# Linear attention's masked scores times values, and attention scores over 32 rows, in single precision without split operands

## The chip, the cores and the metric

The kernel runs on one core of one Trainium2 chip. The metric is the device time of one execution in microseconds, lower is better. All times here come from executions on the chip.

## The reference, cut to what matters

64 batches, each with 64 tokens of 256 features, pass three layers with residual connections: cross attention over a context of 256 rows (16 heads of 16), a gated linear attention (16 heads, keys of 8, values of 16), and a mixture of seven experts and a shared one. The change touches the first two.

```
q, k, v = heads((ln(x) @ Wq + bq)), heads(ctx @ Wk + bk), heads(ctx @ Wv + bv)
attn = softmax(mask(rope(q * 16 ** -0.5) @ rope(k).T))
x = x + (attn @ v) @ Wo + bo
# linear attention, per head and step
state = state * g[..., None] + k[..., :, None] * v[..., None, :]
out = q @ state
x = x + (silu(ln(x) @ Wg + bg) * norm(out)) @ Wo
```

The linear attention is computed in chunks: decayed scores q.k within the 64 steps of a batch, masked to the lower triangle, times the values.

## The kernel before, in words

Each engine has its own hand-written program, and semaphores tie them together. Two batches make a pair, and there are 32 pairs. In one step of the loop every engine does, in an order written out by hand, a part of the attention of pair p, of the linear attention of pair p - 1 and of the projections of pair p + 1. TensorE's order in a step is: scores(p, 0), the turn of the normalised rows for linear attention, the turn of the next context, g_project, project_kv 0, g_gate (the product on line 719 with 16 rows), project_kv 1 to 3, turn_probs(p, 0), g_scores (line 857), turn_xn, weigh_values(p, 0), scores(p, 1), project_q, g_values (line 869), turn_heads(p, 0), turn_k (line 757), turn_probs(p, 1), g_turn_out, weigh_values(p, 1), turn_q (line 777), g_project_out, turn_heads(p, 1), project_out, g_turn_x2, g_logits. Line 714 is every single precision transpose, line 719 every product without split operands, line 727 every split product. After the pairs come the experts, with other code.

A product with split operands has both operands as a half precision high part and a half precision rest: high times high, high times rest, rest times high. Plain operands are single precision, for which the trace shows two records a matmul (one a transpose).

The attention scores (lines 782 to 799). For half b of a pair, four bf16 matmuls put the mask into the four banks ps[:, 0..3, :] (line 788). Then, for two groups g, two parts of the query and four banks r, a matmul over 64 rows (line 796). The 64 rows are two heads, each with the key's high part and its rest side by side; the query's operand holds the high part twice (part 0) or the rest twice (part 1). The query's operand is masked by head parity, so that one matmul gives two heads' scores. What makes those operands:

- key: DVE adds the two rotary products (line 1442), ScalarE casts the high part (k_high, line 1123), GpSimd subtracts the rest (split_k, line 604), TensorE turns 16 half precision blocks (line 757), ScalarE copies two tiles of 128x1024 (k_copies, a helper line, 1104).
- query: DVE adds (line 1456), ScalarE casts twice side by side (q_high, line 1134), DVE subtracts (q_low, line 1460), TensorE turns 8 blocks (line 777), DVE masks the high part in two instructions (line 1470), ScalarE masks the rest (q_low_turned, line 1144).

Masked scores times values in linear attention. DVE masks the scores into a_t in four instructions (line 1584), ScalarE casts a_s[0] (line 1226), GpSimd subtracts a_s[1] (split_a, line 610). DVE makes the values' high part (line 1517) and their rest (line 1522), with the gate's sum between them (line 1519). TensorE does 16 heads x 3 products x 2 batches (line 869), each 64x64 weights and 16 columns. ScalarE copies the result out and undoes the scales of the halves (line 1234), which releases DVE's statistics (lines 1604 to 1621).

GpSimd's step is: residual, masks_of, rope_k (line 591), split_a, split_k, rope_q (line 619), split_v (line 599), split_x2. DVE's step after line 1584 is: line 1442, normalise(p, 0) (lines 1482 and 1490), the gate times its inverse (line 1593), max_rows(p, 1) (line 1416), q_bias (lines 1447 and 1450), the statistics (1604 to 1621), probs_low(p, 1) (line 1476), line 1460, normalise(p, 1), line 1470, and then the sum x2 (line 1635) and its statistics. ScalarE's step after line 1226 is: a copy, line 1123, the exponentials of half 1 and rank 0 (line 1163), the copy on line 1234, the other exponentials with heads_copy between them, lines 1243 and 1246, probs_high(p, 1) (helper line 1104) with line 1134 in its middle, a copy, k_copies, heads_copy, line 1144, the logarithm and exponential of x2's normalisation (lines 1109 and 1112).

Of the kernel before, what the change touches and what calls it, by code (L numbers as in the profile page):

```python
# [51 lines left out]
V_SCALE = 2.0 ** 4  # L52
A_SCALE = 2.0 ** 6
# [14 lines left out]
def constants():  # L68
# [27 lines left out]
    put("gla", (np.arange(SQ)[None, :] >= (p % SQ)[:, None]) * (A_SCALE / W_SCALE ** 2))  # L96
# [65 lines left out]
def program(nc, stack, x, ctx_in, pad, xWq, xbq, xWk, xbk, xWv, xbv, xWo, xbo, gWq, gWk, gWg1, gWg2, gWv,  # L162
# [40 lines left out]
    def halves(k, n):  # L203
# [13 lines left out]
    ident_h1 = place(P // 2).bitcast(F16)  # L217
# [11 lines left out]

    k_s = k_swap.rearrange("p t n -> p (t n)").bitcast(F16).rearrange("p (t h s c) -> p t h s c", t=4, h=8, s=2)  # L230
    k_t = place(4 * 2 * SK // 2).bitcast(F16).rearrange("p (m b j) -> p m b j", m=4, b=2)
# [5 lines left out]

    q_s = q_both.bitcast(F16).rearrange("p (s h r c) -> p s h r c", s=2, h=8, r=2)
    q_t = [place(4 * 2 * 2 * SQ // 2).bitcast(F16).rearrange("p (m b a i) -> p m b a i", m=4, b=2, a=2)
           for _ in range(2)]  # L240
# [12 lines left out]
    g_v_s = halves(1, D)  # L253
# [18 lines left out]
    a_s = [h.rearrange("p r (h c t) -> p r h c t", h=4, c=NCH) for h in halves(4, 4 * NCH * CH)]  # L272
# [82 lines left out]
    for name in """  # L355
# [5 lines left out]
        exp_done probs_turned probs_hi_ready probs_lo_ready v_split v_hi_ready a_hi_ready k_hi_ready k_split q_hi_ready q_split q_lo_t_ready g_v_hi_ready av_done inv_ready av_ready  # L361
# [8 lines left out]
        silu_ready hid_ready down_done y_ready a_split gla_hi_ready gla_lo_ready gs_step decay_step  # L370
# [160 lines left out]
    def _(pool):  # L531
# [5 lines left out]
        nc.gpsimd.tensor_copy(ident_h1, ident).then_inc(S["fill_ready"], 1)  # L537
        pool.wait_ge(S["fill_ready"], 2)
# [62 lines left out]
        def split_k(j):  # L601

            wait(pool, S["k_hi_ready"], j.n(1, 1))
            nc.gpsimd.tensor_tensor(k_s[:, :, :, 1, :], k_rot.rearrange("p t (h c) -> p t h c", h=8),
                                    k_s[:, :, :, 0, :], ALU.subtract).then_inc(S["k_split"], 1)

        def split_a(g):

            wait(pool, S["a_hi_ready"], g.n(1, 1))
            nc.gpsimd.tensor_tensor(a_s[1], a_t, a_s[0], ALU.subtract).then_inc(S["a_split"], 1)  # L610

# [17 lines left out]
        def step(p, nxt=True, gla=True):  # L629
            residual(p)  # L630
            if nxt:
                masks_of(p.next())
                rope_k(p.next())
            if gla:
                split_a(p.next(-1))
            if nxt:
                split_k(p.next())
                rope_q(p.next())
                split_v(p.next())
            if gla:  # L640
                split_x2(p.next(-1))
# [4 lines left out]
        split_k(Step(0, 0))  # L646
# [9 lines left out]
        split_a(Step(0, NPAIR - 1))  # L656
# [52 lines left out]
    def _(pe):  # L709
# [40 lines left out]
        def turn_k(j):  # L750
            wait(pe, S["k_split"], j.n(1, 1))
            for g, bank in enumerate((bank_tb, bank_mb)):
                out = bank.bitcast(F16)
                for m in range(2):
                    for t in range(4):
                        at = (4 * m + t) * P
                        ins = pe.transpose(out[:, at:at + P], k_s[:, t, 4 * g + 2 * m:4 * g + 2 * m + 2, :, :]
                                           .rearrange("p h s c -> p (h s c)"), ident_h1)
                ins.then_inc(S["k_turned"], 1)
# [11 lines left out]
        def turn_q(j):  # L771
            wait(pe, S["q_split"], j.n(1, 1))
            out = bank_ta.bitcast(F16)
            for s in range(2):
                for m in range(4):
                    at = (4 * s + m) * P
                    ins = pe.transpose(out[:, at:at + P],
# [1181 lines left out]
```

## Time and profile before

| | us |
|---|---|
| median of 3 runs | 2202.21 |
| lowest and highest run | 2198.93, 2202.3 |
| the profiled execution | 2206.32 |
| its span, first to last instruction | 2204.5 |
| TensorE busy (matmuls) | 1762.0 (80%) |
| VectorE (DVE) busy | 1489.1 (68%) |
| ScalarE (ACT) busy | 1048.1 (48%) |
| GpSimd (POOL) busy | 746.0 (34%) |
| mean granted TensorE clock, share of full | 0.887 |

PE is TensorE's matmul, PEld its weight load, DVE VectorE, ACT ScalarE, POOL GpSimd. L869 is line 869 of the kernel. In a timeline a row merges neighbouring instructions of one kind: start, length from the first start to the last end, engine, line, operation, what it writes and reads, the count, and in brackets the idle time before it with the releaser. A row of matmuls holds one record for half precision and two for a single precision product. DVE's rows of several instructions overlap a little with the next.

### The profile page before, as it was taken

Reading aid. Unit: us, or ns where it says so; the run is one execution under the profiler, and the core shown is the slowest. Engines: PE = TensorE matmul, PEld = TensorE weight load, DVE = VectorE, ACT = ScalarE, POOL = GpSimd, SP = SyncE. Lnnn points to the kernel's source line nnn. Section 1 sums busy time; section 2 is a strip of 40 time slices with the busy share of each in tenths; the row PEclk is TensorE's granted clock in tenths of the full one; section 3 lists DMA queues with packets and bytes.
Section 4 is the critical chain, followed back from the end, with each engine's and each line's share of the span. In section 5 each row is a group of like instructions: output and inputs, shape, how many; then the busy total and the mean of one; then the engine's idle time right before and its main releaser. Section 6 shows DMA issues by size and latency. Waiting matters only on the chain.

```text
span 2204.5 us, 50620 instructions
## 1 busy us (share of the span) xinstructions
PE 1762.0 (80%) x19164; PEld 1298.4 (59%) x19164; DVE 1489.1 (68%) x2913; ACT 1048.1 (48%) x2616; POOL 746.0 (34%) x850
## 2 busy tenths in 40 slices
PE   5777877787777777877787777656588999999997
PEld 3554555555555555555555555435466888888876
DVE  3777787778877787787877877746554444444446
ACT  2655555555655565555655565532243222222221
POOL 3434333333334332433243324214601333333320
PEclk8988988988889898888889888868889999999999
DMA  3100100010001000100010000003243222222352
GB/s 98 55 17 17 32 17 17 17 32 17 17 17 32 17 17 17 33 17 17 17 32 17 18 17 19 4 3 101 85 114 80 73 71 70 69 72 69 72 178 95
DMA packets 118233, 98.28 MB, mean 45 GB/s; under 512 B 67728, under 2 KB 106272, under 8 KB 118000
## 3 DMA queue, kind: packets, MB, share of 16 engines
q1 hardware_dynamic: 95376, 46.26, 8.3%
q0 software_dynamic: 10752, 33.17, 4.3%
q10 hardware_dynamic: 11872, 15.60, 2.5%
q8 instruction: 163, 2.67, 0.5%
q14 instruction: 70, 0.57, 0.1%
HBM read 62.49 MB, written 18.35 MB: 37 GB/s over the span
## 4 chain that ended last, share of the span: by engine, by line
PE 43%; DVE 16%; issue 6%; ACT 4%; POOL 3%; ACTq 1%; DMA 1%; DVEq 0%; SPq 0%; POOLq 0%
PE ps L1011 15%; PE ps L719 7%; PE ps L1038 7%; PE ps L727 5%; PE ps L714 5%; POOL experts L663 3%; DVE experts L1416 2%; DVE work L1398 2%; DVE experts L1426 1%; ACT experts L1144 1%; PE ps L857 1%; DVE experts L1442 1%; ACT work L1104 1%; PE ps L1043 1%; DVE experts L1584 1%
## 5 line engine op out<-in xcount | busy, mean ns | idle before, releaser
L1011 PE MATMUL ps<-work,experts 128*128 128x256 f16 x3564 | 417.8, 279 | 51.2 <-ACT work L1303 23.4
L1011 PEld LDWEIGHTS ps<-work,experts 128*128 (+1 forms) x3564 | 348.6, 100 | 111.8 <-issue 37.4
L714 PE MATMUL ps<-cst,experts 128*128 128x128 f32 x1376 | 238.6, 313 | 104.9 <-DVE experts L1476 56.7
L1104 ACT ACTIVATE experts<-ps 128x512 f16<-128x512 f32 (+3 forms) x416 | 253.6, 646 | 71.4 <-PE ps L714 67.8
L719 PE MATMUL ps<-experts 128*128 128x512 f32 (+1 forms) x640 | 281.9, 581 | 4.0 <-DMA experts<-in_L_xattn_bv 3.3
L714 PEld LDWEIGHTS ps<-cst,experts 128*128 128x128 f32 x1376 | 177.0, 160 | 155.7 <-issue 91.8
L1163 ACT ACTIVATE experts<-ps,experts 128x256 f32<-128x256 f32 x512 | 235.1, 474 | 64.3 <-DVE experts L1416 64.3
L1104 ACT ACTIVATE work<-work 128x768 f16<-128x768 f32 x108 | 90.9, 842 | 339.0 <-PE ps L1043 216.7
L591 POOL TENSOR_TENSOR experts<-experts,cst 128x128 f32<-128x128 f32 x256 | 135.2, 564 | 281.8 <-DVE experts L1426 281.8
L1038 PE MATMUL ps<-experts,work 128*128 (+1 forms) x1620 | 196.5, 274 | 3.7 <-DVE work L1703 3.7
L719 PEld LDWEIGHTS ps<-experts 128*128 128x128 f32 x640 | 119.8, 200 | 120.2 <-issue 103.4
L1476 DVE TENSOR_TENSOR experts<-ps,experts 128x512 f16<-128x512 f32 x256 | 165.5, 683 | 35.6 <-ACT experts L1104 33.1
L1038 PEld LDWEIGHTS ps<-experts,work 128*128 128x128 f16 x1620 | 154.5, 98 | 28.5 <-DVE work L1703 4.1
L673 POOL DMA_INDIRECT work<-token_in,work x76 | 73.9, 972 | 272.5 <-DMA work<-work 252.7
L1686 DVE SCALAR_TENSOR_TENSOR work<-ps,work 128x768 f32<-128x768 f32 x108 | 88.9, 824 | 111.7 <-ACT work L1303 55.9
L1416 DVE TENSOR_REDUCE experts<-ps 128x2 f32<-128x512 f32 x256 | 159.0, 684 | 4.6 <-PE ps L796 3.4
L1104 ACT ACTIVATE work<-ps 128x128 f32<-128x128 f32 (+2 forms) x160 | 55.5, 347 | 194.6 <-PE ps L714 194.6
L1426 DVE TENSOR_TENSOR experts<-ps,experts 128x512 f32<-128x512 f32 x128 | 88.3, 690 | 77.3 <-PE ps L719 77.3
L719 PE MATMUL ps<-experts,work 128*128 128x256 f32 (+1 forms) x384 | 114.9, 425 | 30.4 <-ACT work L1104 30.4
L1699 DVE TENSOR_TENSOR work<-work 128x768 f16<-128x768 f32 x108 | 91.6, 849 | 60.7 <-ACT work L1104 60.7
L1303 ACT ACTIVATE work<-ps 128x768 f32<-128x768 f32 x108 | 87.2, 807 | 83.4 <-PE ps L1011 82.1
L610 POOL TENSOR_TENSOR work<-experts,work 128x1024 f16<-128x1024 f32 x32 | 68.0, 2126 | 169.1 <-ACT work L1226 169.1
(189 smaller groups left out, 3072.2 us busy)
## 6 DMA issues: line engine op xcount, KB each, us to landing
experts<-in_ctx SPq DMA_DIRECT2D x32, 512.0 KB, 4.6
experts<-choice_out POOLq DMA_DIRECT2D x8, 1024.0 KB, 12.5
experts<-in_x SPq DMA_DIRECT2D x32, 128.0 KB, 2.1
token_in<-experts SPq DMA_DIRECT2D x32, 128.0 KB, 1.7
work<-in_L_ffn_routed_gate ACTq DMA_DIRECT2D x8, 352.0 KB, 2.9
work<-in_L_ffn_routed_up ACTq DMA_DIRECT2D x8, 320.0 KB, 4.5
out<-x_all POOLq DMA_DIRECT2D x5, 512.0 KB, 3.4
experts<-in_L_ffn_routed_gate ACTq DMA_DIRECT2D x6, 352.0 KB, 2.8
```

The lines of the kernel that those rows point to most:

```text
L591: ins = nc.gpsimd.tensor_tensor(dst[:, :, :, e], src[:, :, :, 1 - e], bc(sin[:, t, :, e], 1, H), ALU.mult)
L714: ins = pe.transpose(bank[:, k * P:(k + 1) * P], a, ident)
L719: ins = pe.matmul(bank, lhs[k], rhs[k], start=(k == 0), stop=(k == len(lhs) - 1))
L727: ins = pe.matmul(bank, lhs[a][k], rhs[b][k], start=(k == 0 and a + b == 0), stop=(k == len(lhs[0]) - 1 and a == 1))
L1011: ins = pe.matmul(out, experts_h[:, e, lo:lo + P], e_rows_t[k][:, b * DK + kk, :], start=(kk == 0 and a + b == 0), stop=(kk == DK - 1 and ...
L1038: pe.matmul(out, e_hid_s[a][:, c, rows], experts_h[:, e, at:at + D], start=(c == 0 and a + b == 0), stop=False)
L1104: nc.scalar.activation(dst, src, ACT.Copy).then_inc(done, 1)
L1163: nc.scalar.activation(probs[b][:, 2 * r + g, :], ps[:, r, g * SK:(g + 1) * SK], ACT.Exp, bias=neg_max[b][:, hp:hp + 1], accum_out=row_sum ...
L1416: v.tensor_reduce(nm[:, :, r], ps[:, r, :].rearrange("p (g j) -> p g j", g=2), AX.X, ALU.max, negate=True).then_inc(S["max_ready"], 1)
L1426: v.tensor_tensor(kv[:, t, :], bank, b_kv, ALU.add).then_inc(S["kv_ready"], 1)
L1476: v.tensor_tensor(probs_s[1][:, r, :], probs_bank(b, r), probs_s[0][:, r, :], ALU.subtract)\
L1699: ins = v.tensor_tensor(low, e_hid[:, 0:n], high, ALU.subtract)
```

## The change

The attention scores' and the masked product's operands are single precision. turn_k turns k_rot itself (8 blocks), turn_q turns q_rot itself (2 blocks). The scores run over 32 rows (two heads of 16) in four row groups, 8 matmuls of 256 columns for each half of a pair. k_high, q_high, q_low, q_low_turned, split_k, split_a, the cast a_s[0] and the rest of the values go. The copies of the turned key are two of 128x512. g_values waits for the masking itself and has 32 matmuls. g_gate waits also for the gate's sum, as the gate's sum is now the last reader of its bank. GpSimd no longer makes a half precision identity at the start. Scales of the halves go from the constants. A cut diff:

```diff
-    put("gla", (...) * (A_SCALE / W_SCALE ** 2))
+    put("gla", (...) * (1.0 / W_SCALE ** 2))
-    k_t = place(4 * 2 * SK // 2).bitcast(F16).rearrange("p (m b j) -> p m b j", m=4, b=2)
+    k_t = place(2 * 2 * SK).rearrange("p (g b j) -> p g b j", g=2, b=2)
-    q_t = [place(4 * 2 * 2 * SQ // 2).bitcast(F16)... for _ in range(2)]
+    q_t = place(2 * 2 * 2 * SQ).rearrange("p (g b a i) -> p g b a i", g=2, b=2, a=2)
-    g_v_s = halves(1, D)
+    g_v = place(D)
...
     # GpSimd, def step
-            if gla:
-                split_a(p.next(-1))
-            if nxt:
-                split_k(p.next())
+            if nxt:
                 rope_q(p.next())
                 split_v(p.next())
...
         def turn_k(j):
-            wait(pe, S["k_split"], j.n(1, 1))
+            wait(pe, S["k_rot_ready"], j.n(1, 1))
             for g, bank in enumerate((bank_tb, bank_mb)):
-                for m in range(2):
-                    for t in range(4):
-                        ins = pe.transpose(out[:, at:at + P], k_s[:, t, 4 * g + 2 * m:4 * g + 2 * m + 2, :, :]..., ident_h1)
+                turn(bank, [k_rot[:, t, g * P:(g + 1) * P] for t in range(4)], S["k_turned"])
...
         def turn_q(j):
+            wait(pe, S["q_rot_ready"], j.n(1, 1))
+            turn(bank_ta, [q_rot[:, g * P:(g + 1) * P] for g in range(2)], S["q_turned"])
...
         def scores(p, b):
-            wait(pe, S["q_lo_t_ready"], p.n(1, 1))
+            wait(pe, S["q_t_ready"], p.n(1, 1))
...
             for g in range(2):
-                for part in range(2):
-                    for r in range(4):
-                        m = (4 * g + r) // 2
-                        half = slice(64 * (r % 2), 64 * (r % 2) + 64)
-                        ins = pe.matmul(ps[:, r, g * SK:(g + 1) * SK],
-                                        q_t[part][half, m, b, :, :]..., k_t[half, m, b, :], ...)
+                for r in range(4):
+                    rows = slice(32 * r, 32 * r + 32)
+                    ins = pe.matmul(ps[:, r, g * SK:(g + 1) * SK], q_t[rows, g, b, :, :]...,
+                                    k_t[rows, g, b, :], start=False, stop=(g == 1))
...
         def g_gate(g):
             wait(pe, S["g_v_ready"], g.n(1, 1))
+            wait(pe, S["gate_ready"], g.n(1, 1))
...
         def g_values(g):
-            wait(pe, S["a_split"], g.n(1, 1))
+            wait(pe, S["a_ready"], g.n(4, 4))
             for h in range(H):
-                for k, m in ((0, 0), (0, 1), (1, 0)):
-                    for b in range(2):
-                        ins = pe.matmul(..., a_s[k][rows, h // 4, h % 4, :, :]..., g_v_s[m][rows, 0, ...], ...)
+                for b in range(2):
+                    ins = pe.matmul(..., a_t[rows, h // 4, h % 4, :, :]..., g_v[rows, ...], start=True, stop=True)
...
     # ScalarE, def step
-                wait(act, S["a_ready"], g.n(4, 4))
-                nc.scalar.activation(a_s[0], a_t, ACT.Copy).then_inc(S["a_hi_ready"], 1)
-                k_high(j)
-                nc.scalar.activation(g_out, bank_ma[:, 0:D], ACT.Copy, scale=1 / (A_SCALE * V_SCALE))
+                copy(g_out, bank_ma[:, 0:D], S["go_ready"])
-                q_high(j)
-                q_low_turned(j)
...
     # VectorE, def step
-                v.tensor_scalar(g_v_s[0][:, 0, :], bank_tb[:, 0:D], V_SCALE / W_SCALE, None, ALU.mult)
+                v.tensor_scalar(g_v, bank_tb[:, 0:D], 1 / W_SCALE, None, ALU.mult).then_inc(S["g_v_ready"], 1)
-                v.scalar_tensor_tensor(out=g_v_s[1][:, 0, :], ...)
-                q_low(j)
...
         def q_heads_split(j):
-            src = bank_ta.bitcast(F16)[:, 0:4 * P]...
+            src = bank_ta[:, 0:2 * P].rearrange("p (g b i) -> p g b i", g=2, b=2)
             for a in range(2):
-                ins = v.tensor_scalar(q_t[0][:, :, :, a, :], src, const("par")[:, a:a + 1], None, ALU.mult)
+                ins = v.tensor_scalar(q_t[:, :, :, a, :], src, const("par")[:, a:a + 1], None, ALU.mult)
```

## Rows read from the trace of the kernel before

**Rows 1.** Busy time by stretch, all engines, then granted clock, DMA share, GB/s.

```profile
60.00:1450.00 1390.00, 1070.54 (x13322) 737.32 (x13317) 1094.20 (x2297) 816.51 (x2307) 502.94 (x582) 0.87 0.07 21
```

**Rows 2.** Timeline of DVE in one pair, and one row twelve pairs later.

```profile
818.14 1.67 DVE L1593 TENSOR_TENSOR work<-work 128x256 f32<-128x256 f32 x1
819.85 2.48 DVE L1416 TENSOR_REDUCE experts<-ps 128x2 f32<-128x512 f32 x4
...
826.61 2.65 DVE L1476 TENSOR_TENSOR experts<-ps,experts 128x512 f16<-128x512 f32 x4
...
1350.63 1.68 DVE L1593 TENSOR_TENSOR work<-work 128x256 f32<-128x256 f32 x1
```

**Rows 3.** Line 1593: durations in ns, shortest, median and longest.

```profile
L1593 DVE TENSOR_TENSOR work<-work x32: 414/1672/1680, 100.2 to 1471.4; 128x256 f32<-128x256 f32 x32
```

**Rows 4.** Timeline of POOL in the same pair.

```profile
817.41 2.13 POOL L610 TENSOR_TENSOR work<-experts,work 128x1024 f16<-128x1024 f32 x1 [4.33 <-ACT work L1226]
```

**Rows 5.** Timeline of PE in the same pair.

```profile
817.15 1.93 PE L796 MATMUL ps<-experts 64*128 64x256 f16 x16
...
820.25 1.69 PE L869 MATMUL ps<-work 64*64 64x16 f16 x96
```

**Rows 6.** Timeline of ACT in the same pair.

```profile
821.98 0.38 ACT L1234 ACTIVATE work<-ps 128x256 f32<-128x256 f32 x1 [0.38 <-PE ps L869]
...
825.87 1.06 ACT L1104 ACTIVATE experts<-ps 128x512 f16<-128x512 f32 x2
...
833.65 1.26 ACT L1144 ACTIVATE experts<-ps,cst 128x512 f16<-128x512 f16 x2
834.79 0.30 ACT L1109 ACTIVATE work<-work,cst 128x1 f32<-128x1 f32 x1
```

**Rows 7.** Timelines of PE and DVE, two pairs later.

```profile
907.12 1.05 PE L796 MATMUL ps<-experts 64*128 64x256 f16 x16
...
910.03 1.69 PE L869 MATMUL ps<-work 64*64 64x16 f16 x96 [0.80 <-POOL work L610]
...
910.20 1.89 DVE L1416 TENSOR_REDUCE experts<-ps 128x2 f32<-128x512 f32 x3
```

**Rows 8.** Timeline of PE: short groups at the upper clock, of other shapes and types.

```profile
94.32 0.91 PE L857 MATMUL ps<-work 32*64 32x64 f32 x64
...
822.59 1.06 PE L757 MATMUL ps<-experts 128*128 128x128 f16 x16
...
829.37 1.43 PE L727 MATMUL ps<-work,experts 128*128 128x32 f16 x48 [2.11 <-issue]
...
833.17 0.27 PE L714 MATMUL ps<-cst,work 128*128 128x128 f32 x1
...
836.89 0.61 PE L719 MATMUL ps<-experts,work 128*128 128x7 f32 x4 [0.47 <-ACT work L1104]
...
840.39 1.05 PE L714 MATMUL ps<-cst,experts 128*128 128x128 f32 x8
```

**Rows 9.** Timeline of PE: the turn of the query at either clock.

```profile
787.73 0.61 PE L777 MATMUL ps<-experts 128*128 128x128 f16 x8
...
830.63 1.01 PE L777 MATMUL ps<-experts 128*128 128x128 f16 x8
```

**Rows 10.** Timeline of PE: the first scores of a pair at the lower clock.

```profile
882.98 1.91 PE L796 MATMUL ps<-experts 64*128 64x256 f16 x16
884.82 0.69 PE L714 MATMUL ps<-cst,work 128*128 128x128 f32 x2
```

**Rows 11.** Timelines of POOL and PE ahead of the first pair.

```profile
30.58 2.00 POOL L604 TENSOR_TENSOR experts<-experts 128x1024 f16<-128x1024 f32 x1 [0.81 <-ACT experts L1123]
...
38.61 1.03 PE L788 MATMUL ps<-experts 64*128 64x512 bf16 x4 [2.62 <-ACT experts L1104]
```

**Rows 12.** Timeline of PE: the masked product of the last two pairs.

```profile
1438.01 1.79 PE L869 MATMUL ps<-work 64*64 64x16 f16 x96 [1.85 <-POOL work L610]
...
1474.99 2.73 PE L869 MATMUL ps<-work 64*64 64x16 f16 x96 [4.96 <-issue]
```

More of the change, by code:

```diff
@@ L771, in turn_q @@
         def turn_q(j):
[L772 to L777, printed above, removed]
-                                       q_s[:, s, 2 * m:2 * m + 2, :, :].rearrange("p h r c -> p (h r c)"), ident_h1)
-            ins.then_inc(S["q_turned"], 1)
+            wait(pe, S["q_rot_ready"], j.n(1, 1))
+            turn(bank_ta, [q_rot[:, g * P:(g + 1) * P] for g in range(2)], S["q_turned"])
         def scores(p, b):
@@ L790, in scores @@
             for g in range(2):
-                for part in range(2):
-                    for r in range(4):
-                        m = (4 * g + r) // 2
-                        half = slice(64 * (r % 2), 64 * (r % 2) + 64)
-                        ins = pe.matmul(ps[:, r, g * SK:(g + 1) * SK],
-                                        q_t[part][half, m, b, :, :].rearrange("p a i -> p (a i)"),
-                                        k_t[half, m, b, :], start=False, stop=(g == 1 and part == 1))
+                for r in range(4):
+                    rows = slice(32 * r, 32 * r + 32)
+                    ins = pe.matmul(ps[:, r, g * SK:(g + 1) * SK], q_t[rows, g, b, :, :].rearrange("p a i -> p (a i)"),
+                                    k_t[rows, g, b, :], start=False, stop=(g == 1))
             ins.then_inc(S["scores_done"], 1)
@@ L899, in step @@
                 wait(pe, S["probs_lo_ready"], p.n(8))
-                wait(pe, S["q_lo_t_ready"], p.n(1, 1 if att else 0))
+                wait(pe, S["q_t_ready"], p.n(1, 1 if att else 0))
                 g_turn_x(g)
@@ L920, in step @@
                 wait(pe, S["x1_ready"], p.n(1))
-                wait(pe, S["q_lo_t_ready"], p.n(1, 1))
+                wait(pe, S["q_t_ready"], p.n(1, 1))
                 if gla:
@@ L1119, in ctx_copies @@
                 copy(ctx_t[:, k, :], bank, S["ctx_t_ready"])
-        def k_high(j):
-            wait(act, S["k_rot_ready"], j.n(1, 1))
-            nc.scalar.activation(k_s[:, :, :, 0, :], k_rot.rearrange("p t (h c) -> p t h c", h=8), ACT.Copy)\
-                .then_inc(S["k_hi_ready"], 1)
         def v_high(j):
@@ L1151, in k_copies @@
                 wait(act, S["k_turned"], j.n(2, g + 1))
-                copy(k_t[:, 2 * g:2 * g + 2, :, :].rearrange("p m b j -> p (m b j)"), bank.bitcast(F16),
-                     S["k_t_ready"])
+                copy(k_t[:, g, :, :].rearrange("p b j -> p (b j)"), bank, S["k_t_ready"])
         def exps(p, b, r):
@@ L1658, in _ @@
         q_add(zero)
-        q_low(zero)
         q_heads_split(zero)
```

73 lines of the change are left out of this document (9 added, 64 removed).

## The prediction

> **What bounds the kernel now.** I read the stretches by window first. From 60 to 1450 us, where the kernel works pair by pair, TensorE is busy 1071 us of 1390, VectorE 1094, ScalarE 817 and GpSimd 503 [rows 1]: no engine is full, so the pace is set by a chain that passes from one engine to the next. A pair takes (1350.63 - 818.14) / 12 = 44.4 us, counted over twelve starts of one VectorE line [rows 2]. The steps come in a repeating three: three make 133.1 us, two of them 910.20 - 819.85 = 90.35 [rows 2, 7], so the third is 42.8. They are told apart by which records meet TensorE's lower granted clock (1.2 in place of 2.4 GHz). After 1480 us the experts' part runs, which the diff doesn't touch.
>
> Then I followed the chain of waits through one pair and looked at each place where a removed operation stands on it. There are three.
>
> First, the end of the masked scores of linear attention. ScalarE casts them, GpSimd subtracts (line 610, 2.13 us from 817.41 [rows 4]), and while that runs VectorE's product on line 1593 takes 1.67 us, which takes 0.41 us at its shortest [rows 2, 3]. The reader should see that 1593 ends with GpSimd's instruction, and that the row maxima of the second half (line 1416) start only then, at 819.85, although the scores ended at 817.15 + 1.93 = 819.08 [rows 2, 5].
>
> Second, the end of a pair: TensorE turns the query (line 777), ScalarE makes the second masked query (line 1144) and only then the logarithm of the next normalisation (line 1109) [rows 6, 9].
>
> Third, TensorE itself, where the first scores of a pair stand ahead of the turn that the chain waits for.
>
> **Scores over 32 rows.** Now 16 half precision matmuls take 1.05 us at the upper clock and 1.93 us at the lower [rows 5, 7]. After, 8 single precision ones take two records each, 16 records as before. A single precision record streams a column in twice the time, but four row groups work side by side where there were two. That four do so is shown by line 857, single precision over 32 rows: 64 records in 0.91 us [rows 8], 14 ns each, although each streams 64 columns at twice the time. So the streams cost the same. What is added is a change from 64-row to 32-row tiles after the mask matmuls, with a first weight load that nothing hides. A single precision load of 128 columns is bounded by four records with 7 columns: (0.61 - 0.27) / 3 = 0.11 us [rows 8], where 0.27 is a lone record's length. I take +0.2 us at the upper clock and +0.35 at the lower; the bounds are 0 (the load is hidden) and +0.45/+0.85 (each of the four rounds shows its load).
>
> **Masked scores times values.** Now 96 half precision records of 16 columns take 1.69 us, two side by side: 1.69 / 48 = 35 ns a round [rows 5]. After, 64 records, 32 rounds. They are so short that the weight load sets the round. Half of the 0.11 us above (64 columns in place of 128) and a few ns of stream give 0.06 us, so 32 x 0.06 + 0.15 = 2.0 to 2.1 us. Bounds: 32 x 35 ns = 1.1 us if the load costs no more than now, 2.4 us if load and stream add fully. I take 2.05, the row with the same kind of operand: 0.35 us more than now, with a third fewer instructions.
> The Trainium skill, TensorE: Matmul & The Clock Gate, section "LDWEIGHTS (loading the stationary operand)", gives a load by its columns alone, columns / 1.2, whatever the type. By it the rounds would keep their length and the product would shrink to about 1.1 us. The rows speak against it: 48 half precision records with 128-column weights and 32 columns take 1.43 us, 30 ns each, the single precision ones with 7 columns 110 ns [rows 8].
>
> **The first place.** Lines 610 and 1226 go, line 1593 takes its 0.41 us. In two pairs of three (the scores at the lower clock) the maxima would then start at scores' end, 819.08 + 0.35 = 819.45 in place of 819.85. But the product behind them ends later: 0.25 (the scores; part of the rest now falls in the upper clock) + 0.35, so ScalarE's copy on line 1234 moves from 821.98 to about 822.6 [rows 6]. ScalarE takes the remaining exponentials in order behind that copy, and the first cast of the probabilities behind those, now at 825.87; VectorE's line 1476 starts on that cast, now at 826.61 [rows 2, 6]. So it starts near 827.1: a loss of 0.5 us. In the third kind of pair the scores end at 907.12 + 1.05 = 908.17, the maxima start at 910.20, and the product waits for GpSimd until 910.03 [rows 7]. Here VectorE is last: without the block it gains 1.26 us, of which the exponentials, now behind a product that starts 0.7 us earlier and takes 0.35 longer, let about 0.95 through. Mean over three: (-0.5 - 0.5 + 0.95) / 3, nothing.
>
> **The second place.** Turning the query: 8 half precision transposes take 0.61 us at the upper clock and 1.01 at the lower [rows 9]; two single precision ones take 2 x 0.13 or 2 x 0.26, from eight in 1.05 us [rows 8]. Turning the key stays: 16 in 1.06 us against 8 in 1.05 [rows 8]. Line 1144's 1.26 us ends at 834.91, and 1109 starts at 834.79; the statistics that it also needs are there at about the same time, so of the 1.26 us only what TensorE saves comes through: 0.15 us (upper clock) to 0.43 (lower, which two pairs of three meet). Mean 0.33 gained. Lines 1460, 1123, 604, 1134, 1522 and half of the key's copy are costed at nothing: each ends before something that TensorE or VectorE already waits for otherwise; with that cover gone VectorE's 1460 alone would be 0.6 us.
>
> **The third place.** In one pair of three the first scores run at the lower clock, and the turn of line 714 starts at 884.82 right behind them (882.98 + 1.91) [rows 10]: 0.35 us lost there, a mean of 0.1. The added wait on the gate sum in front of line 848 is met before (the product behind the projections is still queued).
>
> So a steady pair gains 0 + 0.33 - 0.1 = 0.2 us; 29 of them 6 us.
>
> **Once only.** At the start, the casts (1123, 1134) and subtractions (604 from 30.58 to 32.58, 1460) stand ahead of the first scores at 38.61 [rows 11]. Without them, TensorE turns query and key from about 30.4 to 33 and the scores start near 34: 4.5 us gained. At the end, the last two pairs' product waits for GpSimd (1.85 and 4.96 us idle [rows 12]); the first gives 1.85 - 0.4 = 1.4, the second 3.4 (the subtraction's 2.13, the cast ahead of it and their hand-overs) less 1.2 for the longer product at the lower clock, 2.2. Together 8 us.
>
> **Sum.** 6 + 8 = 14 us. The profiled execution took 2206.32 us, the median of the runs is 2202.21, 4.1 less; I set the 14 us against the first and carry them to the second: 2188 us.
>
> **Rivals.** *Full gain (0.2).* The product doesn't get longer, so VectorE's block is the whole price: 0.7 us in two of three (819.85 to 819.15), 1.25 in the third, 0.33 at the second place: 1.2 x 29 + 8 = 43 us, 2159. For: 1593's three quarters of wasted time stand right ahead of the maxima. Against: the 7-column records. The rule of the Trainium skill above leads here.
> *The rhythm holds (0.2).* The falls of the clock return every three pairs with the same sum; if a small gain only shifts which record meets the lower clock, the mean pair stays 44.4 us and only the 8 us remain: 2194. For: twelve periods agree so closely. Against: the three steps differ by some us, so a shift can also break the pattern either way.
> *Slower (0.17).* TensorE's single precision weight loads show in every round of the scores, +0.45 or +0.85 us, twice a pair. Then the first place loses 1.35 in two of three and gains 0.5 in the third, the third place loses 0.85 in one of three: -0.7 -0.3 + 0.33 = -0.7 us a pair, 20 us, less 8: 2214. It decides from about 0.5 us a pair that TensorE needs more than I take, half of that a draw with before. For: the short rounds of 7 columns. Against: 857 hides its loads.
> *No concurrency (0.03).* If the four row groups worked in turn, the scores would take four times 0.87 us: 5 us a pair, over 2300. 857's 14 ns a record speak against it.
>
> **Numbers.** My case has 0.4. Range 2160 to 2210: from the full gain to near the slower case. 0.2% of the time is 4.4 us, about what a measurement of this kernel can tell. Faster than 2197.8: the full gain, most of my case and of the rhythm's: 0.63. Within 0.2%: the upper ends of these two and the mild end of the slower case: 0.19. Slower: 0.18.
>
> **What would show it.** GpSimd's busy time in the pair stage falls by 32 x 4 us, ScalarE's by some us a pair, and the total hardly moves. Line 1593 takes 0.41 us. The product's 64 records take 2.0 us: at 1.1, the full gain. The scores' 16 records take 1.05 to 1.3 us at the upper clock: at 1.5 the slower case. The period of 1593 tells of the rhythm. I am wrong if the maxima of the second half don't start at scores' end, or if the first cast of the probabilities isn't what VectorE then waits for.

## The result, and the profile after

The changed kernel takes 2165.1 us (median of four runs, 2162.12 to 2169.49), the kernel before 2202.26 us in the same session. The ratio is 0.9836, 95% interval 0.9816 to 0.9855: 37 us faster. The forecast was 14 us; the time lies inside the range, near the rival "full gain" (2159), though not for that rival's reason. The profiled execution took 2165.49 us with a span of 2163.7.

Busy time by stretch of the kernel after; the columns are those of [rows 1].

```profile
60.00:1450.00 1390.00, 1120.72 (x12025) 764.49 (x12025) 1035.79 (x2263) 680.22 (x2157) 371.73 (x521) 0.84 0.07 21
```

Against [rows 1] GpSimd lost 131 us, ScalarE 136 and VectorE 58, as the removed instructions should. The stretch is as long as before, but 0.7 of a pair more fits into it. So TensorE's 50 us more overstate it: over the same 29 pairs (96.87 to 1391.94 us before, 90.29 to 1357.10 after) it is busy 1038.4 us in place of 1003.8, 1.2 us *more* a pair, while the pair got shorter. The mean clock is lower too (0.84 against 0.87). Neither tells the time of this kernel. Whether it counts which records meet the lower clock is what the experiments ask.

The lines have moved: the scores are now line 754, the masked product 826, the gate product 1506 (was 1593), the maxima 1339, the low half of the probabilities 1394, ScalarE's copies 1061. Shortest, median and longest durations in ns of the gate product, and the single precision product's matmul records:

```profile
L1506 DVE TENSOR_TENSOR work<-work x32: 415/425/427, 93.6 to 1435.9; 128x256 f32<-128x256 f32 x32
...
L826 PE MATMUL ps<-work,experts x2048: 206/206/283, 96.2 to 1439.5; 64*64 64x16 f32 x187
```

VectorE's product is no longer held up by GpSimd ("the block" below) in any pair (before 414/1672/1680, [rows 3]). Now one pair with the second half's scores at the upper clock, and the pair after the next, with them at the lower clock. Timeline of PE:

```profile
840.15 1.15 PE L754 MATMUL ps<-experts 32*128 32x256 f32 x16
842.29 2.04 PE L826 MATMUL ps<-work,experts 64*64 64x16 f32 x64
...
925.94 2.09 PE L754 MATMUL ps<-experts 32*128 32x256 f32 x16
929.44 2.04 PE L826 MATMUL ps<-work,experts 64*64 64x16 f32 x64
```

Timeline of DVE in the same two pairs:

```profile
841.41 0.42 DVE L1506 TENSOR_TENSOR work<-work 128x256 f32<-128x256 f32 x1
841.87 2.49 DVE L1339 TENSOR_REDUCE experts<-ps 128x2 f32<-128x512 f32 x4
...
848.63 2.47 DVE L1394 TENSOR_TENSOR experts<-ps,experts 128x512 f16<-128x512 f32 x4
...
883.80 0.43 DVE L1506 TENSOR_TENSOR work<-work 128x256 f32<-128x256 f32 x1
...
926.98 0.42 DVE L1506 TENSOR_TENSOR work<-work 128x256 f32<-128x256 f32 x1
928.09 2.49 DVE L1339 TENSOR_REDUCE experts<-ps 128x2 f32<-128x512 f32 x4 [0.69 <-PE ps L754]
...
935.77 2.48 DVE L1394 TENSOR_TENSOR experts<-ps,experts 128x512 f16<-128x512 f32 x4
...
971.11 0.43 DVE L1506 TENSOR_TENSOR work<-work 128x256 f32<-128x256 f32 x1
```

The scores' 16 records take 1.15 and 2.09 us (before 1.05 and 1.93, [rows 5, 7]), the product 2.04 in both (before 1.69). At the lower clock the maxima wait for the scores (0.69 us idle); at the upper clock nothing holds them but VectorE's own order: they start at 841.87, 0.57 us after the scores' end. (The prediction called itself wrong if they don't start at scores' end; at the upper clock they don't quite.) From line 1506 to line 1394 it is 848.63 - 841.41 = 7.22 us at the upper clock and 935.77 - 926.98 = 8.79 at the lower. In the kernel before, the same stretch took 826.61 - 818.14 = 8.47 us [rows 2], and as much in the upper-clock pairs, since the block was there in both.

The pattern of three is still there, with other steps. The starts of line 1506 give 883.80 - 841.41 = 42.39 and 926.98 - 883.80 = 43.18; the third step is 971.11 - 926.98 = 44.13, together 129.7 us (before 133.1). And the mix has turned: before, one pair of three had these scores at the upper clock, now two of three have.

Where the 40.8 us of span went, from the starts of the masking instruction (line 1584 before, 1497 after) in the second pair and 29 pairs later: 96.87 and 1391.94 before, 90.29 and 1357.10 after. Up to the second pair 6.6 us; 29 steps 28.3 us (0.97 each); from there to the end of the last masked product 3.1 us (1474.99 + 2.73 before, [rows 12]; 1436.20 + 3.60 after); the experts' part, which is the same code, 2.9 us. (That last is no gain of the change: over the five traces of each kernel with equal delays, below, this part takes 725.4 us before and 725.0 after, between 723.6 and 727.3.) First scores and last product of the kernel after, timeline of PE:

```profile
34.20 2.09 PE L754 MATMUL ps<-experts 32*128 32x256 f32 x16
...
1436.20 3.60 PE L826 MATMUL ps<-work,experts 64*64 64x16 f32 x64 [1.67 <-issue]
```

### The profile page after: what moved, and what is told of

It is laid out like the page before. It is cut to its first block, busy times and chain, and to the rows that moved or that the text cites. A ratio compares the mean times of both kernels' runs of the same rounds, so it can differ in the third digit from the quotient of the medians.

```text
span 2163.7 us, 47324 instructions
## 1 busy us (share of the span) xinstructions
PE 1799.0 (83%) x17692; PEld 1317.2 (61%) x17692; DVE 1419.3 (66%) x2849; ACT 904.3 (42%) x2456; POOL 609.9 (28%) x785
## 4 chain that ended last, share of the span: by engine, by line
PE 64%; DVE 17%; issue 8%; ACT 5%; POOL 3%; DMA 1%; ACTq 1%; SPq 0%; DVEq 0%; POOLq 0%
PE ps L968 15%; PE ps L692 15%; PE ps L687 11%; PE ps L700 7%; PE ps L995 7%; PE ps L754 3%; POOL experts L636 3%; PE ps L826 2%; DVE experts L1349 2%; DVE work L1321 2%; DVE experts L1394 2%; ACT experts L1061 1%; PE ps L749 1%; ACT work L1061 1%; DVE work L1487 1%
## 5 line engine op out<-in xcount | busy, mean ns | idle before, releaser
L687 PE MATMUL ps<-cst,experts 128*128 128x128 f32 x1696 | 299.3, 328 | 111.2 <-DVE experts L1394 57.1
L687 PEld LDWEIGHTS ps<-cst,experts 128*128 128x128 f32 x1696 | 240.3, 170 | 157.9 <-issue 98.5
L1061 ACT ACTIVATE experts<-ps 128x512 f16<-128x512 f32 (+2 forms) x416 | 223.6, 580 | 92.7 <-PE ps L687 88.5
L1061 ACT ACTIVATE work<-ps 128x128 f32<-128x128 f32 (+1 forms) x192 | 67.3, 351 | 267.8 <-PE ps L687 223.6
L692 PE MATMUL ps<-experts,work 128*128 128x256 f32 (+1 forms) x384 | 128.8, 467 | 30.4 <-ACT work L1061 30.4
L700 PE MATMUL ps<-experts 128*128 128x32 f16 x2560 | 89.3, 180 | 58.2 <-issue 54.0
L700 PEld LDWEIGHTS ps<-experts 128*128 128x128 f16 x2560 | 84.4, 98 | 69.4 <-issue 61.0
```

The lines of the kernel that those rows point to most:

```text
L687: ins = pe.transpose(bank[:, k * P:(k + 1) * P], a, ident)
L692: ins = pe.matmul(bank, lhs[k], rhs[k], start=(k == 0), stop=(k == len(lhs) - 1))
L700: ins = pe.matmul(bank, lhs[a][k], rhs[b][k], start=(k == 0 and a + b == 0), stop=(k == len(lhs[0]) - 1 and a == 1))
L1061: nc.scalar.activation(dst, src, ACT.Copy).then_inc(done, 1)
```

## The experiments

Three theories stood at first, and the expectations name them. **A:** the block by GpSimd was the price of the old kernel, and taking it away is the gain. **B:** the gain came from the rest: the shorter turn of the query, ScalarE's missing casts, the missing wait for GpSimd's result. **C:** the clock's pattern sets the mean pair, whatever is changed, and allows only a few values. Each time stands beside the kernel before of the same session (2201.6 to 2203.4). "Way" below is the time from the start of the masking instruction to the first subtraction of the second half's probabilities, a mean over 25 pairs from the fifth on; "upper" is in how many of these the second half's scores ran at the upper clock. Both, and "pair", the mean step over the same 25 pairs, are read from the timelines of one execution of each run. Three of these lie off the median of their run: the one of the block put back took 2185.76 us, the one without the block 2215.3, the late cast of the values 2166.22. The kernel before has a way of 11.83 us and 9 upper pairs, the one after 11.11 and 16.

### The block put back

In the changed kernel GpSimd gets a subtraction of the old shape (128x1024) at the old place, its result unused:

```
+            if nxt and gla:
+                wait(pool, S["inv_ready"], p.n(2, 1))
+                nc.gpsimd.tensor_tensor(spare_h, spare, spare, ALU.subtract)
```

> The kernel after, with one GpSimd subtraction of 128x1024 on constant data put back where the rest of the masked scores was made (released by the reciprocal of the row sums, so that it starts about when it did before); nothing waits for its result. Theory A (the block of VectorE's product by GpSimd was most of the price): the product gate times inverse takes about 1.6 us again, the maxima of the second half start 5.0 us after the masking's start in every pair, the mean pair goes from 43.2 to about 44.0 us and the time to about 2188. Rival B (the gain came from the shorter turn of the query, the missing casts on ScalarE and the missing wait for GpSimd's result): the time stays within 5 us of 2165. Rival C (the rhythm of three pairs with the clock sets the mean pair, whatever is changed): the mean pair is one of few values, 43.2 or 44.4.

Measured: 2190.9 us (2185.76 to 2191.36), ratio 0.9948, 0.9931 to 0.9965. A pair with its scores at the upper clock, timelines of PE and DVE:

```profile
849.40 1.15 PE L763 MATMUL ps<-experts 32*128 32x256 f32 x16
...
850.66 1.59 DVE L1515 TENSOR_TENSOR work<-work 128x256 f32<-128x256 f32 x1
852.29 2.49 DVE L1348 TENSOR_REDUCE experts<-ps 128x2 f32<-128x512 f32 x4
...
859.04 1.28 DVE L1403 TENSOR_TENSOR experts<-ps,experts 128x512 f16<-128x512 f32 x2
```

The scores end at 850.55, but the maxima start at 852.29, behind the blocked product. 18 of 25 pairs are upper, and it does nearly nothing for them: their way is 11.71 us (10.54 in the changed kernel), the mean of all 25 11.83 us as before. By the ratios 25 us of the 37 are gone. A's number came out, B's did not. But the time alone doesn't decide between A and C: the mean pair is 44.17 us, near C's 44.4, and two other small edits of the changed kernel that put no block back (one logarithm, one cast, below) cost 24 and 26 us. What this run shows for A is the way in the upper pairs.

### The block taken out of the kernel before

Line 1593 is moved ahead of line 1442, before GpSimd's subtraction starts; nothing else changes.

```
+                v.tensor_tensor(gate_i, gate, gate_i, ALU.mult)
             if nxt:
                 k_add(j)
             if att:
                 normalise(p, 0, bank_mb)
-                v.tensor_tensor(gate_i, gate, gate_i, ALU.mult)
```

> The kernel before, with VectorE's product gate times inverse moved ahead of the rotary sum of the key, where GpSimd is idle; nothing else. Theory A: 0.4 us in place of 1.67, a gain of 0.5 to 1.2 us a pair, 2175 to 2180. Rival B: within 5 us of 2202, since the masked product's end (the copy of its result) comes no earlier. Rival C: the mean pair goes to 43.2 us (2167) or stays at 44.4 (2202).

Measured: 2208.03 us (2201.69 to 2215.3), ratio 1.0018, 1.0006 to 1.0029. A misses by 30 us; B and C's second value, 44.4 us a pair (44.58 in this trace), come near. The way did shrink, to 11.44 us, but the four subtractions behind it stretched from 2.69 to 2.95 us (they now wait for ScalarE's casts, with the query's cast in their middle) and the stretch from x1's normalisation to the first key-value bias from 6.53 to 6.86. A gain in one place was given back in two others.

### Each half of the change alone

Product alone: a_t and the values in single precision, scores as before. Scores alone: the reverse.

> The kernel before with the masked product's half of the change alone. Theory A: the key's subtraction on GpSimd now starts after the product gate times inverse, so the block is gone with it; the masked product takes 2.04 us; 2175 to 2180, most of the whole gain. Rival B: about 2195, since the query's and key's casts are still there.

> The kernel before with the attention scores' half of the change alone. Theory A: the block stays at 1.67 us, since the subtraction that causes it is the masked scores'; the start of the kernel gives 5 us, the turn of the query and the casts 0.5 us a pair less 0.15 for the longer scores: 2185 to 2192. Rival B: 2170, most of the whole gain.

Measured: product alone 2196.62 us (ratio 0.9977, 0.9966 to 0.9987), scores alone 2197.79 (0.9976, 0.9966 to 0.9986). A misses both, by 17 us and by 6; B has the first and misses the second by 28. By the ratios the halves bring 5 us each, and both together bring 36. Product alone, timelines of PE and DVE:

```profile
545.74 1.94 PE L787 MATMUL ps<-experts 64*128 64x256 f16 x16
...
590.12 1.94 PE L787 MATMUL ps<-experts 64*128 64x256 f16 x16
...
634.50 1.94 PE L787 MATMUL ps<-experts 64*128 64x256 f16 x16
```

```profile
546.74 0.43 DVE L1576 TENSOR_TENSOR work<-work 128x256 f32<-128x256 f32 x1
...
591.12 0.43 DVE L1576 TENSOR_TENSOR work<-work 128x256 f32<-128x256 f32 x1
```

There is no block, but every pair, 44.38 us after the last, meets the lower clock at the same scores; 3 of 25 pairs are upper. Scores alone, timelines of PE, POOL and DVE:

```profile
808.39 1.15 PE L765 MATMUL ps<-experts 32*128 32x256 f32 x16
811.19 1.69 PE L837 MATMUL ps<-work 64*64 64x16 f16 x96 [0.59 <-POOL work L596]
...
808.92 2.13 POOL L596 TENSOR_TENSOR work<-experts,work 128x1024 f16<-128x1024 f32 x1 [4.81 <-ACT work L1173]
...
809.65 1.67 DVE L1525 TENSOR_TENSOR work<-work 128x256 f32<-128x256 f32 x1
811.36 2.49 DVE L1353 TENSOR_REDUCE experts<-ps 128x2 f32<-128x512 f32 x4
```

All 25 pairs are upper, but the block stays and the way is 11.78. One half removes the block and has nearly no fast pairs, the other has only fast pairs and keeps the block. A short way needs both: an unblocked pair whose scores are at the upper clock. That the short way then also gives a short kernel does not follow, as the next experiment shows.

### A small delay, in both kernels

If the time hangs on the pattern of the clock, a tiny edit off this place must have a large effect. The edit: k more 128x1 logarithms ahead of x2's on ScalarE, results unused. By the start of the two normalisations around it, one costs 0.18 us a pair, two 0.36, three 0.55, four 0.74.

```
         def rstd(k, which, n, m):
             wait(act, S[which + "_stat_ready"], n)
+            for extra in range(EXTRA if k == 2 else 0):
+                nc.scalar.activation(spare_l[:, extra:extra + 1], stats[k][:, 7:8], ACT.Ln, bias=const("eps"))
```

> The changed kernel with one more 128x1 logarithm ahead of x2's on ScalarE, at most 0.3 us on the chain of each pair, nothing else. If each pair pays what is put on its chain, the time rises by 0 to 8 us, to 2165 to 2174, in steps of three pairs that each grow by up to 0.9 us. If the time is set by which pairs meet the lower clock, the pattern of 129.7 us for three either holds its length or breaks up: then the change is far from linear, under 0 or over 15 us.

> The changed kernel with four more such logarithms, at most 1.2 us on the chain of each pair. Linear: four times what one costs, up to 35 us (to 2200). Set by the clock: another ratio than four to one, and another mix of second-half scores at the upper and the lower clock than two to one.

> The kernel before with one more 128x1 logarithm ahead of x2's on ScalarE; the same edit cost the changed kernel 0.19 us at its place and 24.6 us in all. If the changed kernel's pattern of three is the special case and the kernel before is at the usual pace of 44.4 us a pair, it pays what the place costs, 31 x 0.19 = 6 us, or less: 2202 to 2210. If the kernel before owes its own time to a pattern of three in the same way, the edit moves it by over 10 us in either direction.

> The kernel before with four more such logarithms, 0.73 us at their place in each pair (as in the changed kernel with the same edit). Every pair pays: 31 x 0.73 = 23 us, 2225. The lower clock gives part back where the pair is longer: 2205 to 2218; the changed kernel with this edit went to 2199.15, so between the two kernels 6 to 19 us would be left of 37.

> The changed kernel with two more logarithms, about 0.37 us at their place. One cost 24.6 us and four 34.1. If the special pattern, once lost, gives way to the usual pace, two lie between them: 2190 to 2199, a mean pair of 44.2 to 44.4. If patterns come and go with the length of the pair, it may be anything from 2165 to 2200, below the run with one.

> The kernel before with two more logarithms (0.36 us at their place). The same place cost it 5.0 us with one and 40.5 with four. By the length of the chain alone 31 x 0.36 = 11 us: 2213; with the shifts of the clock 2200 to 2225. Against the changed kernel with the same edit, 2186.02, the change is then worth 14 to 39 us; 14 if its lasting part is what was forecast, about 30 if it is the mean of the differences so far (37, 17, 43).

> The kernel before with three more logarithms (0.55 us at their place): by length alone 17 us, 2219; between the runs with one and four 2207 to 2242.

> The changed kernel with three more logarithms. With one, two and four it took 2189.75, 2186.02 and 2199.15. By length alone from the unchanged one, 2165 + 17 = 2182; from the runs beside it 2188 to 2197. The difference to the kernel before with the same edit is 14 us if the forecast was the lasting part of the change, 30 us or more if it was too small in every rhythm.

Measured, both kernels with the same delay (us; pair, way and upper as defined above; before / after; the last column is the difference of the two ratios, each to the kernel before of its own session):

```
logarithms   time before / after   pair            way             upper     difference
0            2202.26 / 2165.10     44.39 / 43.29   11.83 / 11.11    9 / 16   1.64%
1            2206.58 / 2189.75     44.44 / 44.20   11.83 / 11.60   15 /  9   0.79%
2            2224.31 / 2186.02     44.97 / 44.10   11.81 / 11.25   21 / 14   1.74%
3            2225.34 / 2198.76     45.06 / 44.39   11.77 / 10.53   24 / 25   1.28%
4            2242.09 / 2199.15     45.59 / 44.28   11.77 / 10.85   24 / 20   2.07%
mean         2220.1  / 2187.8      44.89 / 44.05   11.80 / 11.07   93 / 84   1.50%
```

Four readings. First, one logarithm, 0.18 us a pair or 6 us in all, costs the changed kernel 24 us by the ratios, and the second costs it nothing more (21 for both; the difference is within the intervals). The kernel before pays 5 us for one, as expected, but 42 for four, by the ratio, where the length alone gives 23; it and the changed kernel with three (2198.76, expected up to 2197) lie outside what was expected. With one, a long stretch of pairs meets the lower clock at the same scores every 44.37 us; timelines of PE and DVE:

```profile
538.77 2.09 PE L755 MATMUL ps<-experts 32*128 32x256 f32 x16
...
583.14 2.09 PE L755 MATMUL ps<-experts 32*128 32x256 f32 x16
...
539.60 0.43 DVE L1509 TENSOR_TENSOR work<-work 128x256 f32<-128x256 f32 x1
...
583.97 0.43 DVE L1509 TENSOR_TENSOR work<-work 128x256 f32<-128x256 f32 x1
```

That is the picture of the product alone.

Second, this pace is no accident of one kernel. The changed kernel with three logarithms repeats after three pairs, with four after five, each for at least 15 pairs; timelines of DVE, first with three, then with four:

```profile
767.13 0.43 DVE L1509 TENSOR_TENSOR work<-work 128x256 f32<-128x256 f32 x1
...
900.26 0.43 DVE L1509 TENSOR_TENSOR work<-work 128x256 f32<-128x256 f32 x1
```

```profile
458.09 0.42 DVE L1509 TENSOR_TENSOR work<-work 128x256 f32<-128x256 f32 x1
...
679.96 0.42 DVE L1509 TENSOR_TENSOR work<-work 128x256 f32<-128x256 f32 x1
```

(900.26 - 767.13) / 3 = 44.38 and (679.96 - 458.09) / 5 = 44.37 us a pair. The kernel before has 44.37 over twelve pairs [rows 2], the product alone 44.37, the cast put back (below) 88.75 for two. So kernels whose ways run from 10.53 to 11.83 us keep one pace, and the changed kernel takes 0.18 to 0.74 us of delay a pair without leaving it. Over all 25 pairs, with their irregular steps, the delayed ones have 44.10 to 44.39. Clearly faster are only the changed kernel as it stands, with 129.7 / 3 = 43.24, and the two versions at the end of this part (43.27 and 42.80, without a pattern that lasts). The kernel before leaves 44.37 sooner: in the stretches that repeat it takes 44.95 with two logarithms and 45.50 with four. So theory C has a part in every time here, though with more values than its two. Much of the 37 us is therefore the pattern that this one kernel fell into. What the change gives beside it is room: it holds the old pace with up to 0.74 us more on the chain, where the kernel before has lost it at 0.36.

Third, the kernel before keeps a way of 11.8 us whether 9 or 24 of its pairs are upper, while the changed kernel's follows its count of upper pairs. With three logarithms nearly all pairs of both are upper. Kernel before, where the gate product is blocked (1.67 us) and the maxima start behind it, timelines of PE and DVE:

```profile
825.30 1.05 PE L797 MATMUL ps<-experts 64*128 64x256 f16 x16
...
823.36 1.41 DVE L1587 TENSOR_TENSOR experts<-ps,cst 128x256 f32<-128x256 f32 x4
...
826.66 1.67 DVE L1596 TENSOR_TENSOR work<-work 128x256 f32<-128x256 f32 x1
828.37 2.49 DVE L1419 TENSOR_REDUCE experts<-ps 128x2 f32<-128x512 f32 x4
835.13 2.66 DVE L1479 TENSOR_TENSOR experts<-ps,experts 128x512 f16<-128x512 f32 x4
```

Changed kernel, the same:

```profile
855.72 1.15 PE L755 MATMUL ps<-experts 32*128 32x256 f32 x16
...
853.68 1.41 DVE L1500 TENSOR_TENSOR experts<-ps,cst 128x256 f32<-128x256 f32 x4
...
864.20 2.47 DVE L1397 TENSOR_TENSOR experts<-ps,experts 128x512 f16<-128x512 f32 x4
```

835.13 - 823.36 = 11.77 us against 864.20 - 853.68 = 10.52.

Fourth, the five differences have a mean of 1.50%, 33 us, between 17 and 46. The 14 us of the forecast lie below the smallest. No theory holds alone: some 33 us are the mean worth of the change over these five delays (an estimate, from 20 to 46 us by their scatter, if five delays are a fair sample of the patterns), and the pattern adds or takes up to 16.

### The query's cast put back

The forecast costed line 1134 at nothing. Here a 128x512 cast of 0.63 us stands again in the middle of ScalarE's casts of the second half's probabilities, its result unused:

```
-                probs_high(p, 1)
+                probs_high(p, 1, 0, 2)
+                nc.scalar.activation(spare_q, bc(q_rot.rearrange("p (h c) -> p h c", h=8), 2, 2), ACT.Copy)
+                probs_high(p, 1, 2, 4)
```

> The changed kernel with the query's high cast (a 128x512 cast of 0.64 us) put back in the middle of ScalarE's four casts of the second half's probabilities, its result unused. The prediction costed its removal at nothing. If that was right the time stays at 2165. If it was on the chain, the four subtractions of line 1394 stretch from 2.48 to about 2.9 us, 0.2 to 0.4 us a pair, 6 to 12 us by themselves: 2171 to 2177, unless the clock's mix turns too.

Measured: 2192.82 us (2186.73 to 2195.8), ratio 0.9952, 0.9938 to 0.9967. Timeline of DVE, one pair:

```profile
642.32 1.29 DVE L1400 TENSOR_TENSOR experts<-ps,experts 128x512 f16<-128x512 f32 x2
643.91 1.29 DVE L1400 TENSOR_TENSOR experts<-ps,experts 128x512 f16<-128x512 f32 x2 [0.29 <-ACT experts L1062]
```

VectorE now waits for ScalarE between the second and the third subtraction; the four stretch from 2.48 to 2.83 us in the mean. That is 0.35 us a pair, 10 us of the 26 by the ratios, and not nothing. The other 16 go with the pattern: the steps alternate between 46.40 and 42.35 us, again 44.37 in the mean, and 12 pairs are upper in place of 16.

### A faster version

In the changed kernel VectorE's normalisation of x1 is itself blocked, by GpSimd's split of the values (1.70 us for 0.41); durations in ns:

```profile
L1321 DVE TENSOR_SCALAR work<-work x32: 414/1703/1708, 70.2 to 1419.3; 128x256 f32<-128x256 f32 x32
```

Moving ScalarE's cast of the values behind x1's logarithm and exponential undoes that. The second kernel also moves line 1506 ahead of the key's sum.

```
-            if nxt:
-                v_high(j)
             if gla:
                 wait(act, S["logits_done"], p.n(1))
...
             if att:
                 rstd(1, "x1", p.n(1, 1), norm_count(p, 2))
+            if nxt:
+                v_high(j)
```

> The changed kernel, with ScalarE's high cast of the values moved behind the logarithm and exponential of x1's normalisation. In the changed kernel GpSimd's split of the values runs while VectorE applies x1's normalisation, which takes 1.70 us where 0.41 us is its shortest. If VectorE's wait is on the chain in every pair, the pair loses 1.29 us at that place and up to 0.6 us more, since ScalarE no longer makes the cast ahead of x1's logarithm: 29 x 1.3 to 1.9 = 38 to 55 us, 2110 to 2127. Rival (the clock takes it back): the gain at this place is there in the trace, but the mix of clocks turns, and between none and half of it is left: 2140 to 2165.

> The changed kernel with the values' high cast behind x1's normalisation (2154.92 by itself), and with VectorE's product of line 1506 moved ahead of the key's sum, since in pairs whose scores run at the upper clock the maxima start 0.57 us after the scores' end, behind VectorE's work. At its place it gains 0.4 us in such pairs, part of which ScalarE's order keeps: up to 0.2 us a mean pair, 2148 to 2155, if the mix of clocks stays; with another mix 2140 to 2185.

Measured: 2154.92 us (2150.31 to 2166.22), ratio 0.9784, 0.9765 to 0.9803; and 2156.63 (2149.23 to 2160.51), 0.9798, 0.977 to 0.9825. x1's normalisation in the first of them, durations in ns:

```profile
L1321 DVE TENSOR_SCALAR work<-work x32: 411/414/415, 70.7 to 1420.0; 128x256 f32<-128x256 f32 x32
```

The block is gone in all 32 pairs, and the stretch from x2's normalisation to the end of x1's shrank by 1.38 us (4.64 to 3.26). The stretch behind it grew by 1.0 (6.43 to 7.44), and only 8 pairs are upper (way 11.63). This execution took 2166.22 us, as long as the changed kernel; the other four took 2150 to 2156. So its trace shows that the block is gone and where the time went back, but not where the 10 us of the median come from. They are what is left of the 40 that the place alone would give in 29 pairs: the rival in this expectation was nearer, and its upper half holds the time. The first version beats the changed kernel (the intervals don't overlap). The second brings nothing at its place: the way is 10.54 us in its upper pairs and 12.14 in the others, as in the changed kernel. Its time doesn't differ from the first version's, and its interval touches the changed kernel's.

## Why the prediction was right or wrong

**Direction and bound: right.** It is a chain through the engines; GpSimd's block on line 1593 stood right ahead of the maxima, and putting it back lengthens the way of the upper pairs from 10.54 to 11.71 us. (It costs 25 us in all, but so do edits without a block.)

**The sizes of the two products: right.** The masked product was put at 2.05 us and takes 2.04. The scores were put at +0.2 and +0.35 us and take +0.10 and +0.16 more, inside the bounds. The Trainium skill, TensorE: Matmul & The Clock Gate, section "LDWEIGHTS (loading the stationary operand)", gives a load of 64 columns 64 / 1.2 = 53 ns: by that figure, an estimate, the 32 rounds take 1.7 us. The 1.1 us of the prediction come from its reading that the type plays no part, and from the old rounds of 35 ns. The trace agrees with neither: 64 records in 2.04 us are 64 ns a round, and the old rounds, with 64 columns too, take 35 ns. How much of the 64 ns is load and how much streaming no run separates.

**Once only: right.** The first scores start at 34.20 us (forecast 34). The masking of the second pair starts 6.6 us earlier; over the five equal delays the mean is 94.55 - 89.45 = 5.1 (forecast 4.5). The end brings 3.1 (forecast 3.6). The 2.9 us of the experts' part are scatter: 0.3 us are left in the mean of five.

**The second place: about right.** From the last subtraction to x2's normalisation the five kernels before take 6.06 us in the mean, the five after 5.86: 0.20 us, forecast 0.33. The third place was put at -0.1; from the end of x1's normalisation to the next masking 0.28 are lost.

**The first place: the step that failed**, in "Mean over three: (-0.5 - 0.5 + 0.95) / 3, nothing". It takes the mean pair for a sum of prices, weighted with the mix of one trace, two pairs at the lower clock to one at the upper. The prices were of the right kind and order. Over all five delays a pair at the lower clock goes from a way of 11.89 us to 12.16 (-0.27, forecast -0.5), one at the upper from 11.77 to 10.54 (+1.23, forecast +0.95). With the forecast's own weights these prices give 0.2 us in place of nothing; the rest is the weights. The changed kernel has 16 upper pairs of 25, and the mix moves with small delays that touch no operation of the change: the kernel before has 9, 15, 21, 24 and 24 upper pairs with 0 to 4 logarithms more. Over all five the changed kernel has 84 of 125, so the place is worth 11.80 - (0.67 x 10.54 + 0.33 x 12.16) = 0.73 us in the mean; in the kernel as it stands 11.83 - 11.11 = 0.72. In the kernel before the upper pairs could not pay off, because the block outlasted the scores at either clock.

The weighting itself is only an account of means. For a single kernel it doesn't give the time: with three logarithms the changed kernel's way is the shortest of all (10.53 us, all pairs upper), and its pair takes the old 44.37 us. The kernel as it stands leaves that pace for 43.24. Why it does, and why its next neighbour with 0.18 us more doesn't, stays open.

**A cover that was none.** Line 1134 was costed at nothing as ending ahead of work that is waited for otherwise. It stood between ScalarE's casts: the four subtractions take 2.67 us in the mean of the five before and 2.48 after, 0.19 us.

Together a pair gains 0.73 + 0.19 + 0.20 - 0.28 = 0.84 us in the mean of the five delays in place of 0.2, 24 us in 29 pairs; with 5.1 and 3.1 once only that is 32 us, near the 33 of the mean difference. The kernel as it stands got 37, of which 28 in the pairs, by its pattern: that this comparison and the mean lie so near is luck, as one logarithm more leaves 17.

**The rivals.** "The rhythm holds" had the mechanism, a small shift that moves which records meet the lower clock, and a mean pair that stays at 44.4 with 8 us once only. For the changed kernel with any of the four delays the pace did stay near it (44.10 to 44.39 over 25 pairs); the kernel as it stands fell out of it, to 43.24, as the rival's own "against" allowed. "Full gain" had the number (2159), but from a product that does not get longer, and it does: luck. "Slower" and "no concurrency" fell with the scores' 1.15 us.

## What to carry to other kernels

Where TensorE's clock falls at places that change from step to step, price an edit for each clock apart, and don't take the mix from one trace: give the weights a range of their own. Before believing a gain or a loss of a per cent, add the same small harmless delay in several sizes to both kernels and compare the means; here a single comparison gave anything from 17 to 46 us for one change. Look for a pace that several variants share: here it was 44.37 us a pair, and an edit that only moves a kernel onto or off such a pace says little of the place it was made at. An instruction that outlasts its partner at either clock hides the clock, so that the two halves of a change can be worth far less apart than together (5 and 5 us against 36).

## What the runs showed of the hardware that was not expected

One logarithm, 0.18 us on the chain of each pair, cost 24 us over 32 pairs, and two cost 21: the time of this periodic kernel is far from linear in its work. The pace locks: the kernel before, the product alone, the cast put back and the changed kernel with one, three or four logarithms all run long stretches at 44.37 us a pair in the mean, with patterns of one, two, three or five pairs that repeat to a few hundredths of a us, though their ways differ by up to 1.3 us. And a lower mean clock (0.84 against 0.87) went with the shorter time. What makes the clock fall at those records, and what fixes the pace, was not tried.
